# A fused attention and feed-forward kernel: layer 1's order on TensorE, and the start of the program, are rearranged

## The chip, the cores and the metric

The kernel runs on one core of a Trainium2 chip. The metric is device time in microseconds (us) of one execution, as the median of repeated runs. The core has TensorE (PE in the rows, its weight loads PEld), VectorE (DVE), ScalarE (ACT), GpSimd (POOL) and SyncE (SP), which here only issues transfers. Each engine works through its own instruction list in order; they meet at semaphores.

## The reference

Sixteen sequences of 512 tokens and 128 channels go through one attention block and one feed-forward block, each with its input added and normalised over the channels:

```python
normed = rms_norm(x, gamma)
q, k, v = normed @ w_q * 16**-0.5, *split(normed @ w_kv)     # 8 heads of 16
q, k = taylor(q), taylor(k)                                  # 1, x, x_i x_j / sqrt 2
out = (q @ (k^T v)) / max(q . sum(k), 1e-5)                  # linear attention
x = layernorm(x + out @ w_out)
h = silu(x @ w1^T * s1) * (x @ w2^T * s2)                    # 128 -> 512
h = gelu(h @ h1^T * hs1); h = gelu(h @ h2^T * hs2)           # 512 -> 512, twice
x = layernorm(x + h @ w3^T * s3)                             # 512 -> 128
```

All arrays are fp32. The weights w1, w2, h1, h2 and w3 are drawn from -1, 0 and 1 and multiplied by 8.

## The kernel before, in words

One sequence is one batch. The work of a batch is cut into four stages, and step t of the program does front of batch t, middle of t-1, ffn of t-2 and tail of t-3. Steps 0, 1 and 2 are written out, steps 3 to 14 run in a loop of two steps per pass, and 15 to 18 are written out again. Within a step the instructions of every engine stand in an order fixed by hand (`step` of each engine). The table RING names, in order, the uses of four PSUM banks by front and middle; FPS does the same for the four banks of ffn and tail. From these tables each wait is worked out: who writes a bank waits until its last content was read.

Front: x is scaled (`xn`), transposed (`xT`), multiplied by w_kv and w_q (`kv0` to `kv3`, `qT`); nine products with 0/1 matrices (`sq0` to `sq8`) form sums of q that ScalarE squares into `phiT`; `state` gathers k and v. Middle: the state of the batch before is transposed (`stateT`, `restT`), applied to phiT (`apply_main`, `apply_rest`, into `acc0`, `acc1`), divided (`normalise`, into `att`), projected (`out`), and x1 is transposed for the ffn (`x1T`). Ffn: layer 1 has a gate product a_m and a linear product b_m for each m of 0 to 3; ScalarE's `silu` reads a_m, VectorE's `gate_mult` multiplies it with b_m, `gate_hi` and `gate_lo` split the result in two parts. Layers 2 and 3 (`two0` to `three3`) end in `gelu` on ScalarE and `gelu_tile` on VectorE; layer 4 writes `y`, and ScalarE's `copy_y` takes it out for `transpose_y` of the next step. b1 and y use the same bank.

An operand that must be more exact than the fast fp32r format is split into a rounded part (`_hi`) and a rest (`_lo`). Activations always have both. For the ffn weights the kernel forms both, sums the absolute rests (`weights_lo_sum`), and TensorE reads the largest sum into a register (`value_load`) and branches: if there is no rest, the third product of each tile is left out. The profiled run goes that way. The three parts of the weights (w1, w2, w3; h1; h2) are loaded into tiles that the steps use later for other things, so their rests must be formed before step 1 goes on.

## Time and profile before

| | us |
|---|---|
| Median of 3 runs | 604.39 (604.31 to 605.26) |
| Profiled execution | 604.67 |
| its span, first to last instruction | 602.9 |
| TensorE, VectorE, ScalarE, GpSimd busy in the span | 559.8, 492.6, 464.5, 145.0 |
| TensorE's granted clock, mean | 0.984 |

The busy time of an engine is the time in which at least one of its instructions ran. Matmuls overlap, so the distance from one start to the next is what a matmul takes from TensorE, not the length in its row. "issue" is time in which an engine waited for nothing that the profile shows.

### The profile page before, as it was taken

To read this page: it belongs to the slowest core of one execution; us is meant where nothing else is said; L and a number is where in the kernel's file an instruction comes from. 1 tells how busy PE (TensorE), PEld (TensorE's weight loads), DVE (VectorE), ACT (ScalarE), POOL (GpSimd) and SP (SyncE) were. 2 spreads that over 40 slices of the span, in tenths; PEclk is the share of its full clock that TensorE was granted. 3 is DMA by queue.
4 is the path that set the end of the run, shared out by engine and by line. 5 is a ranking of instruction groups with operands and counts; after the bars stand their busy time and mean duration, and the time that the engine had idled before them with its cause. 6 is when DMAs were issued, how large, how long until landed. Compare 5 with 4: busy or idle time off the path is not lost.

```text
span 602.9 us, 11637 instructions
## 1 busy us (share of the span) xinstructions
PE 559.8 (93%) x3729; PEld 412.3 (68%) x3729; DVE 492.6 (82%) x1018; ACT 464.5 (77%) x953; POOL 145.0 (24%) x218
## 2 busy tenths in 40 slices
PE   3655999999999999999999999999999999999994
PEld 2334686867768686877868686776868687686772
DVE  5984886979799797979889797979979797987664
ACT  4565788796969788796978879796977969697773
POOL 5522112213212221312312231231132132110100
PEclk9986999999999999999999999999999999999998
DMA  8000000000000000000000000000000000000000
GB/s 277 1 20 3 1 17 3 18 18 18 20 0 17 17 17 17 17 17 17 0 17 17 17 17 17 17 17 0 17 17 17 17 17 17 1 1 18 6 14 35
DMA packets 7368, 12.36 MB, mean 21 GB/s; under 512 B 817, under 2 KB 1841, under 8 KB 7345
## 3 DMA queue, kind: packets, MB, share of 16 engines
q1 hardware_dynamic: 7056, 11.93, 5.8%
q8 instruction: 14, 0.23, 0.2%
q10 hardware_dynamic: 288, 0.13, 0.1%
q14 instruction: 10, 0.07, 0.0%
HBM read 7.86 MB, written 4.19 MB: 20 GB/s over the span
## 4 chain that ended last, share of the span: by engine, by line
PE 64%; ACT 15%; issue 12%; DVE 7%; DMA 1%; SPq 0%; DVEq 0%; POOLq 0%; POOL 0%; ACTq 0%
PE fps L416 20%; PE fps L417 19%; ACT phiT L630 5%; PE ring L395 5%; PE ring L387 5%; PE ring L319 4%; PE ring L342 3%; ACT hid_hi L673 3%; PE ring L403 2%; ACT fps L674 2%; PE ring L326 2%; ACT wide L679 2%; DMA h<-in_h 1%; PE fps L459 1%; ACT x1T_hi L639 1%
## 5 line engine op out<-in xcount | busy, mean ns | idle before, releaser
L416 PE MATMUL fps<-hid_hi,w_hi 128*128 128x512 f32 x576 | 226.8, 394 | 2.4 <-DVE hid_lo L897 1.8
L417 PE MATMUL fps<-hid_lo,w_hi 128*128 128x512 f32 x576 | 226.4, 393 | 0.0
L416 PEld LDWEIGHTS fps<-hid_hi,w_hi 128*128 128x128 f32 x576 | 108.2, 188 | 26.8 <-DVE hid_lo L897 4.1
L673 ACT ACTIVATE hid_hi<-fps,col 128x512 fp32r<-128x512 f32 x128 | 88.2, 689 | 46.3 <-PE fps L417 46.0
L417 PEld LDWEIGHTS fps<-hid_lo,w_hi 128*128 128x128 f32 x576 | 108.3, 188 | 22.4
L897 DVE TENSOR_TENSOR hid_lo<-fps,hid_hi 128x512 fp32r<-128x512 f32 x128 | 87.0, 689 | 24.2 <-ACT fps L674 22.0
L630 ACT ACTIVATE phiT<-ring 128x512 f32<-128x512 f32 x128 | 73.6, 595 | 28.2 <-PE ring L342 28.2
L674 ACT ACTIVATE fps<-fps,col 128x512 f32<-128x512 f32 x128 | 84.4, 660 | 0.0
L883 DVE SCALAR_TENSOR_TENSOR h<-fps,col,gate_zo 128x512 f32<-128x512 f32 x64 | 47.9, 749 | 42.8 <-ACT gate_zo L660 41.4
L259 DVE TENSOR_TENSOR phi_k<-phi_k 128x896 f32<-128x896 f32 x64 | 70.0, 1098 | 1.8 <-ACT v_one L602 1.3
L342 PE MATMUL ring<-qT,sel 128*128 128x512 f32 x128 | 55.3, 442 | 13.6 <-issue 9.0
L416 PE MATMUL fps<-x1T_hi,w_hi 128*128 128x512 f32 x128 | 56.3, 440 | 5.4 <-ACT wide L679 5.4
L1043 POOL TENSOR_TENSOR k_mid<-phi_k,v_one 128x256 f32<-128x256 f32 x32 | 21.4, 667 | 163.1 <-ACT v_one L602 133.2
L660 ACT ACTIVATE gate_zo<-fps,col 128x512 f32<-128x512 f32 x64 | 45.8, 715 | 15.7 <-PE fps L417 15.6
L889 DVE TENSOR_TENSOR hid_lo<-h,hid_hi 128x512 fp32r<-128x512 f32 x64 | 44.0, 687 | 9.2 <-ACT hid_hi L665 7.2
L417 PE MATMUL fps<-x1T_lo,w_hi 128*128 128x512 f32 x128 | 50.4, 394 | 0.0
L1024 POOL TENSOR_TENSOR rn<-ssc,const 128x4 f32<-128x4 f32 x16 | 16.6, 1039 | 129.9 <-DVE ssc L782 129.9
L653 ACT ACT_TABLE_LOAD x33 | 42.3, 1283 | 2.3 <-PEq L1129 1.7
L602 ACT ACTIVATE phi_k<-ring 128x128 f32<-128x128 f32 (+1 forms) x128 | 24.7, 256 | 24.6 <-PE ring L319 24.4
L416 PEld LDWEIGHTS fps<-x1T_hi,w_hi 128*128 128x128 f32 x128 | 24.0, 188 | 28.0 <-issue 12.6
L665 ACT ACTIVATE hid_hi<-h 128x512 fp32r<-128x512 f32 x64 | 42.3, 661 | 1.0 <-DVE h L883 0.9
L342 PEld LDWEIGHTS ring<-qT,sel 128*128 128x128 f32 x128 | 24.8, 198 | 23.9 <-issue 13.3
(107 smaller groups left out, 939.3 us busy)
## 6 DMA issues: line engine op xcount, KB each, us to landing
x_b<-in_x SPq DMA_DIRECT2D x16, 256.0 KB, 2.5
out<-gate_zo SPq DMA_DIRECT2D x16, 256.0 KB, 2.0
h<-in_h SPq DMA_DIRECT2D x1, 1024.0 KB, 8.1
gate_zo<-in_h SPq DMA_DIRECT2D x1, 1024.0 KB, 10.7
wide<-in_w SPq DMA_DIRECT2D x3, 256.0 KB, 3.9
sel_raw<-in_sel SPq DMA_DIRECT2D x1, 384.0 KB, 8.5
w_qkv_raw<-in_w_kv SPq DMA_DIRECT2D x1, 128.0 KB, 2.7
const<-in_consts ACTq DMA_DIRECT2D x1, 115.0 KB, 3.0
```

What stands on the lines that cost most here:

```text
L259: return eng.tensor_tensor(out, fixed, moved, ALU.mult)
L342: mm = nc.tensor.matmul(ring[:, bank, :], sel[:, (f % 4) * P:(f % 4 + 1) * P], qT[f // 4][:, :], start=True, stop=True)
L416: nc.tensor.matmul(fps[:, bank, :], w_hi[:, o:o + P], hi, start=start, stop=False)
L417: mm = nc.tensor.matmul(fps[:, bank, :], w_hi[:, o:o + P], lo, start=False, stop=stop and not with_lo)
L630: op = nc.scalar.activation(phiT[:, f, :], ring[:, bank, :], ACT.Square)
L653: nc.scalar.activation(table_use[:, :], source, function)
L660: nc.scalar.activation(gate[:, m % 2, :], fps[:, bank_of(FPS, f"a{m}"), :], ACT.Silu, scale=s1_c[:, m:m + 1]).then_inc(f_free[bank_of(FPS, ...
L673: nc.scalar.activation(hid[1 - layer][0][:, m, :], fps[:, bank, :], ACT.Gelu, scale=scale)
L674: nc.scalar.activation(fps[:, bank, :], fps[:, bank, :], ACT.Gelu, scale=scale)\
L883: nc.vector.scalar_tensor_tensor(out=h32[:, m, :], in0=fps[:, bank_of(FPS, b), :], scalar=s2_c[:, m:m + 1], in1=gate[:, m % 2, :], op0=ALU ...
L889: nc.vector.tensor_tensor(hid[0][1][:, m, :], h32[:, m, :], hid[0][0][:, m, :].bitcast(F32), ALU.subtract).then_inc(split_ready, 1)
L897: nc.vector.tensor_tensor(lo, fps[:, bank, :], hi.bitcast(F32), ALU.subtract)\
```

## The change

In the loop, TensorE does layer 1 as a0 b0 a1 b1, the three transposes, a2 b2 a3 b3, then `apply_main`, `apply_rest` and `transpose_y` in one piece, and then kv0 and kv1; before, the transposes and the two applies stood between the pairs of layer 1. ScalarE takes out the state and y of the step before first, then does silu 0, sq7, sq6, silu 1 and the copies of the transposed states; before, it copied sq6, sq7 and y ahead of silu 0, in that order. VectorE does phi_k 0 later.

In steps 0 to 2, no rests of weights are formed. The weights have a tile of their own (`w_raw`). ScalarE sums the lower 16 bits of each weight's pattern; TensorE adds these sums over the partitions with one small product, VectorE adds three numbers, and TensorE branches on the result. If it isn't zero, the products are done in full fp32 from `w_raw`. In step 0 ScalarE copies `sel`, and VectorE rounds no weights. `state`, `sq6` and `sq7` of batch 1 move behind the first half of layer 1 of step 2, and h1 is loaded behind `sel` and the second x.

```diff
@@ RING
-    ("stateT", MIDDLE, 0), ("restT", MIDDLE, 1), ("xT", FRONT, 2), ("kv0", FRONT, 3), ("acc0", MIDDLE, 0),
-    ("acc1", MIDDLE, 1), ("kv1", FRONT, 2), ("kv2", FRONT, 3), ("out", MIDDLE, 0), ("qT", FRONT, 1), ("kv3", FRONT, 2),
+    ("stateT", MIDDLE, 0), ("restT", MIDDLE, 1), ("xT", FRONT, 2), ("acc0", MIDDLE, 0), ("acc1", MIDDLE, 1),
+    ("kv0", FRONT, 3), ("kv1", FRONT, 2), ("kv2", FRONT, 3), ("out", MIDDLE, 0), ("qT", FRONT, 1), ("kv3", FRONT, 2),
@@ SyncE
             load_ffn_weights(0, (o1, w1t), (o2, w2t), (o3, w3t))
-            load_ffn_weights(1, (oh1, h1t))
             sp.dma_start(sel_raw[:, :], sel_d).then_inc(sel_loaded, 16)
             peeled(step, 0)
+            load_ffn_weights(1, (oh1, h1t))
             load_ffn_weights(2, (oh2, h2t))
@@ TensorE, product
-                mm = nc.tensor.matmul(fps[:, bank, :], w_hi[:, o:o + P], lo, start=False, stop=stop and not with_lo)
-                if with_lo:
-                    mm = nc.tensor.matmul(fps[:, bank, :], w_lo[:, o:o + P], hi, start=False, stop=stop)
-                return mm
+                if in_full:
+                    nc.tensor.matmul(fps[:, bank, :], w_raw[:, o:o + P], hi.bitcast(F32), start=start, stop=False)
+                    return nc.tensor.matmul(fps[:, bank, :], w_raw[:, o:o + P], lo.bitcast(F32), start=False, stop=stop)
...
@@ TensorE, step
+                    if is_step(t, 2):
+                        for part in range(3):
+                            pe.wait_ge(w_hi_ready[part], 1)
                     if ffn:
                         layer1(t, 0, in_full)
+                        layer1(t, 1, in_full)
+                    if is_step(t, 2):
+                        state(1)
+                        sums_of_q(1, 6)
+                        sums_of_q(1, 7)
                     if middle:
                         transpose_state(t)
-                    if ffn:
-                        layer1(t, 1, with_lo)
-                    if middle:
                         transpose_rest(t)
                     if front:
                         transpose_x(t)
                     if ffn:
                         layer1(t, 2, in_full)
+                        layer1(t, 3, in_full)
                     if middle:
                         apply_main(t)
-                    if ffn:
-                        layer1(t, 3, with_lo)
-                    if front:
-                        project_kv(t, 0)
-                    if middle:
                         apply_rest(t)
                     if tail:
                         transpose_y(t)
                     if front:
+                        project_kv(t, 0)
                         project_kv(t, 1)
@@ TensorE, the start
             pe.wait_ge(consts_loaded, 16)
-            pe.wait_ge(qkv_w_ready, 7)
...
                 apply_main(1)
+                apply_rest(1)
                 project_kv(1, 0)
-                apply_rest(1)
                 project_kv(1, 1)
+                pe.wait_ge(lo_sums_ready, 3)
+                nc.tensor.matmul(fps[0:1, 3, 0:3], half_c, lo_sums[:, :], start=True, stop=True)\
+                    .then_inc(lo_sums_added, 1)
...
-                pe.wait_ge(lo_max_ready, 1)
-                nc.tensor.transpose(fps[0:1, 3, 0:P], lo_max[:, :], ident).then_inc(lo_max_T, 1)
...
-                for f in (0, 1, 8, 2, 3):
-                    sums_of_q(1, f)
                 transpose_x1(1, 0)
-                sums_of_q(1, 4)
-                sums_of_q(1, 5)
-                state(1)
-                sums_of_q(1, 6)
-                sums_of_q(1, 7)
+                for f in (0, 1, 8, 2, 3, 4, 5):
+                    sums_of_q(1, f)
@@ ScalarE
+                low = w_raw[:, a:b].bitcast(mybir.dt.uint16).rearrange("p (n two) -> p n two", two=2)[:, :, 0]
+                nc.scalar.activation(unused[:, 0:b - a], low, ACT.Copy, accum_out=lo_sums[:, part:part + 1])\
+                    .then_inc(lo_sums_ready, 1)
...
             square(0, 0)
+            weights_low_bits(0)
...
             def step(t, par, front, middle, ffn, tail):
-                if ffn:
+                if is_step(t, 2):
                     silu(t, 0)
                 if middle:
-                    ring_copy(t, "stateT", w_main[:, :], ring[:, bank_of(RING, "stateT"), 0:2 * P], half_c)
+                    state_copy(t - 1)
+                if tail:
+                    copy_y(t - 1)
+                if ffn and not is_step(t, 2):
+                    silu(t, 0)
+                if middle:
+                    square_sums(t - 1, 7, 6)
                 if ffn:
                     silu(t, 1)
                 if middle:
+                    ring_copy(t, "stateT", w_main[:, :], ring[:, bank_of(RING, "stateT"), 0:2 * P], half_c)
                     ring_copy(t, "restT", w_rest[:, :], ring[:, bank_of(RING, "restT"), 0:2 * P])
                 if front:
                     x_hi(t)
                 if is_step(t, 0):
+                    act.wait_ge(sel_loaded, 16)
+                    nc.scalar.activation(sel[:, :], sel_raw[:, :], ACT.Copy).then_inc(sel_ready, 1)
+                if is_step(t, 1):
+                    weights_low_bits(2)
                     a, b = w_parts[0]
+                    nc.scalar.activation(w_hi[:, a:b], w_raw[:, a:b], ACT.Copy).then_inc(w_hi_ready[0], 1)
-                if is_step(t, 1):
-                    weights_lo_sum(0)
...
                 if is_step(t, 1):
-                    weights_lo_sum(1)
-                    weights_lo_sum(2)
+                    x1_hi(t)
...
+                if is_step(t, 0):
+                    weights_low_bits(1)
                 if middle:
                     load_table(ACT.Silu)
-                if front:
-                    ring_copy(t, "state", st[:, :, :].rearrange("p g f -> p (g f)"),
-                              ring[:, bank_of(RING, "state"), 0:2 * FEAT])
-                    square_sums(t, 6, 7)
-                if ffn:
-                    copy_y(t)
@@ VectorE, step
                     gate_mult(t, 1)
+                if front:
+                    x_lo(t)
+                if ffn:
                     gate_lo(t, 0)
-                if front:
-                    x_lo(t)
-                if ffn:
                     gate_mult(t, 2)
...
-                if front:
-                    phi_k_main(t, 0)
...
                     gelu_tile(t, 0, 0)
+                if front:
+                    phi_k_main(t, 0)
...
@@ VectorE, first_step
                 x_lo(0)
-                round_weights(dve, nc.vector, 1)
                 phi_k_main(0, 0)
-                dve.wait_ge(sel_loaded, 16)
-                nc.vector.tensor_copy(sel[:, :], sel_raw[:, :]).then_inc(sel_ready, 1)
                 q_lo(0)
@@ VectorE, second_step
-                split_weights(dve, nc.vector, 1)
+                round_weights(dve, nc.vector, 1)
+                x_lo(1)
                 round_weights(dve, nc.vector, 2)
-                split_weights(dve, nc.vector, 2)
-                x_lo(1)
+                normalise(1)
+                dve.wait_ge(lo_sums_added, 1)
+                nc.vector.tensor_reduce(lo_sum[:, :], fps[0:1, 3, 0:3], AX.X, ALU.add).then_inc(lo_sum_ready, 1)
                 phi_k_main(1, 0)
-                dve.wait_ge(w_lo_ready[0], 1)
-                normalise(1)
...
@@ GpSimd
             normed_x(0, 0)
-            split_weights(pool, nc.gpsimd, 0)
             peeled(step, 0)
```

## Rows read from the trace of the kernel before

**Rows 1.** The page: busy time, share of the span and instructions by engine.

```profile
PE 559.8 (93%) x3729; PEld 412.3 (68%) x3729; DVE 492.6 (82%) x1018; ACT 464.5 (77%) x953; POOL 145.0 (24%) x218
```

**Rows 2.** The waits: total us, times, longest.

```profile
PE fps L416 <- ACT wide L679: 5.4, 13, 0.4
```

**Rows 3.** Timeline, TensorE, one loop step: start us, length us, instruction, [idle before].

```profile
265.69 0.40 PE L416 MATMUL fps<-x1T_hi,w_hi 128*128 128x512 f32 x1
...
266.75 0.48 PE L416 MATMUL fps<-x1T_hi,w_hi 128*128 128x512 f32 x1
267.06 0.40 PE L417 MATMUL fps<-x1T_lo,w_hi 128*128 128x512 f32 x1
267.86 0.50 PE L416 MATMUL fps<-x1T_hi,w_hi 128*128 128x512 f32 x1 [0.41 <-ACT wide L679]
268.20 0.40 PE L417 MATMUL fps<-x1T_lo,w_hi 128*128 128x512 f32 x1
...
268.65 0.60 PE L311 MATMUL ring<-const,xn 128*128 128x128 f32 x4
...
272.54 0.39 PE L416 MATMUL fps<-x1T_hi,w_hi 128*128 128x512 f32 x1
...
300.28 0.40 PE L416 MATMUL fps<-x1T_hi,w_hi 128*128 128x512 f32 x1
```

**Rows 4.** Timeline, ScalarE, the same step.

```profile
266.16 1.07 ACT L630 ACTIVATE phiT<-ring 128x512 f32<-128x512 f32 x2
267.11 0.70 ACT L679 ACTIVATE wide<-fps,col 128x512 f32<-128x512 f32 x1
...
268.61 0.72 ACT L660 ACTIVATE gate_zo<-fps,col 128x512 f32<-128x512 f32 x1
```

**Rows 5.** Timeline, VectorE, the fill.

```profile
11.69 4.66 DVE L249 CAST w_hi<-h 128x512 fp32r<-128x512 f32 x4 [1.33 <-DMA h<-in_h]
...
18.69 0.68 DVE L800 TENSOR_TENSOR qT<-ring,qT 64x512 fp32r<-64x512 f32 x1
...
36.00 1.31 DVE L817 STREAM_TRANSPOSE wide<-ring 128x512 f32<-128x512 f32 x2
...
46.72 0.28 DVE L987 TENSOR_REDUCE lo_max<-fps 1x1 f32<-1x128 f32 x1
```

**Rows 6.** Timeline, TensorE, the fill.

```profile
24.04 3.81 PE L359 MATMUL ring<-phi_k,v_one 128*32 128x153 f32 x64
...
30.84 1.93 PE L387 MATMUL ring<-phiT,w_main 128*32 128x512 f32 x16
...
39.56 1.13 PE L403 MATMUL ring<-w_o,att 128*128 128x128 f32 x8 [2.44 <-issue]
...
42.18 0.41 PE L567 MATMUL fps<-const,lo_max 128*1 128x128 f32 x1
51.57 1.19 PE L342 MATMUL ring<-qT,sel 128*128 128x512 f32 x2 [8.97 <-issue]
...
55.90 2.29 PE L359 MATMUL ring<-phi_k,v_one 128*32 128x153 f32 x64
...
68.41 0.39 PE L416 MATMUL fps<-hid_hi,w_hi 128*128 128x512 f32 x1
```

**Rows 7.** Timeline, VectorE, the loop step of rows 3.

```profile
269.37 0.75 DVE L883 SCALAR_TENSOR_TENSOR h<-fps,col,gate_zo 128x512 f32<-128x512 f32 x1 [0.19 <-ACT gate_zo L660]
```

**Rows 8.** The DMA issue under way at 3.1 us: KB each, us to landing.

```profile
wide<-in_w SPq DMA_DIRECT2D x1, 256.0 KB, 4.9
```

**Rows 9.** Timeline, ScalarE, the fill.

```profile
9.04 0.60 ACT L608 ACTIVATE xnT_hi<-ring 128x512 fp32r<-128x512 f32 x1 [5.06 <-PE ring L311]
...
14.45 0.59 ACT L622 ACTIVATE qT<-ring 64x512 fp32r<-64x512 f32 x1 [0.71 <-PE ring L326]
...
31.24 1.48 ACT L648 ACTIVATE hid_lo<-w_lo 128x1536 fp32r<-128x1536 f32 x1
```

**Rows 10.** Stretch by engine: PE, PEld, DVE, ACT, POOL busy, PEclk, DMA, GB/s.

```profile
45.00:52.00 7.00, 0.43 (x1) 0.47 (x2) 5.04 (x10) 0.00 (x0) 1.68 (x3) 0.50 0.01 2
```

More of the change, by code:

```diff
@@ L187, in build @@
         qkv_w_ready = sem("qkv_w_ready")
-        w_hi_ready, w_lo_ready = ([sem(f"{n}{part}") for part in range(3)] for n in ("w_hi_ready", "w_lo_ready"))
-        lo_sums_ready, lo_max_ready, lo_max_T, lo_max1_ready = (
-            sem(n) for n in ("lo_sums_ready", "lo_max_ready", "lo_max_T", "lo_max1_ready"))
+        w_hi_ready = [sem(f"w_hi_ready{part}") for part in range(3)]
+        lo_sums_ready, lo_sums_added, lo_sum_ready = (sem(n) for n in ("lo_sums_ready", "lo_sums_added", "lo_sum_ready"))
         sq_ready, ss_ready, ssc_ready, rn_ready, xn_ready = (
@@ L316, in project_kv @@
                     pe.wait_ge(ring_free[bank_of(RING, "xT")], read(RING, t, "xT"))
+                    if is_step(t, 0):
+                        pe.wait_ge(qkv_w_ready, 7)
                 bank_wait(RING, ring_free, t, f"kv{j}")
@@ L412, in transpose_x1, with product, layer1 @@
                 mm.then_inc(f_full, 1)
-            def product(bank, o, hi, lo, start, stop, with_lo):
+            def product(bank, o, hi, lo, start, stop, in_full):
+                if in_full:
+                    nc.tensor.matmul(fps[:, bank, :], w_raw[:, o:o + P], hi.bitcast(F32), start=start, stop=False)
+                    return nc.tensor.matmul(fps[:, bank, :], w_raw[:, o:o + P], lo.bitcast(F32), start=False, stop=stop)
                 nc.tensor.matmul(fps[:, bank, :], w_hi[:, o:o + P], hi, start=start, stop=False)
-                mm = nc.tensor.matmul(fps[:, bank, :], w_hi[:, o:o + P], lo, start=False, stop=stop and not with_lo)
-                if with_lo:
-                    mm = nc.tensor.matmul(fps[:, bank, :], w_lo[:, o:o + P], hi, start=False, stop=stop)
-                return mm
-            def layer1(t, m, with_lo):
+                return nc.tensor.matmul(fps[:, bank, :], w_hi[:, o:o + P], lo, start=False, stop=stop)
+            def layer1(t, m, in_full):
                 for what, o in ((f"a{m}", o1), (f"b{m}", o2)):
@@ L427, in layer1, with hidden @@
                         pe.wait_ge(f_free[bank_of(FPS, "x1T")], read(FPS, t - 1, "x1T"))
-                    product(bank_of(FPS, what), o + m * P, x1T[0][:, :], x1T[1][:, :], True, True, with_lo)\
+                    product(bank_of(FPS, what), o + m * P, x1T[0][:, :], x1T[1][:, :], True, True, in_full)\
                         .then_inc(f_full, 1)
-            def hidden(t, what, o, wide, src, made_by, m, tiles, with_lo):
+            def hidden(t, what, o, wide, src, made_by, m, tiles, in_full):
                 for k in tiles:
@@ L440, in hidden, with layer2, layer3, layer4 @@
                     mm = product(bank_of(FPS, what), o + k * wide + m * P, hid[src][0][:, k, :],
-                                 hid[src][1][:, k, :], k == 0, k == KT - 1, with_lo)
+                                 hid[src][1][:, k, :], k == 0, k == KT - 1, in_full)
                     if k == KT - 1:
                         mm.then_inc(f_full, 1)
-            def layer2(t, m, tiles, with_lo):
-                hidden(t, f"two{m}", oh1, HID, 0, None, m, tiles, with_lo)
-            def layer3(t, m, tiles, with_lo):
-                hidden(t, f"three{m}", oh2, HID, 1, "two", m, tiles, with_lo)
-            def layer4(t, tiles, with_lo):
-                hidden(t, "y", o3, D, 0, "three", 0, tiles, with_lo)
+            def layer2(t, m, tiles, in_full):
+                hidden(t, f"two{m}", oh1, HID, 0, None, m, tiles, in_full)
+            def layer3(t, m, tiles, in_full):
+                hidden(t, f"three{m}", oh2, HID, 1, "two", m, tiles, in_full)
+            def layer4(t, tiles, in_full):
+                hidden(t, "y", o3, D, 0, "three", 0, tiles, in_full)
             def transpose_y(t):
@@ L532, in step @@
                     if ffn:
[L533 to L534 removed]
+                        layer3(t, 3, (2, 3), in_full)
+                        layer4(t, (0,), in_full)
                     if front:
@@ L704, in step @@
                     gate_hi(t, 2)
+                    gate_hi(t, 3)
                 if front:
                     copy_kv(t, 0)
-                if ffn:
-                    gate_hi(t, 3)
-                if front:
                     copy_kv(t, 1)
@@ L744, in step @@
                     square_sums(t, 3)
-                if middle:
+                if middle and not is_step(t, 1):
                     x1_hi(t)
@@ L908, in step @@
                 if ffn:
+                    gate_lo(t, 0)
                     gate_mult(t, 2)
```

91 lines of the change are left out of this document (37 added, 54 removed).

## The prediction

> **What bounds the kernel now.** I read the page first: TensorE is busy 93% of the span [rows 1], so the time is TensorE's work plus its gaps. The waits tell where the gaps of the loop are: one place has 13 of them, a layer 1 product held by ScalarE's copy of y [rows 2]. Then the timeline of one step. It runs from one a0 to the next, 265.69 to 300.28, 34.59 us [rows 3]. In it b1 starts 0.80 after the product before, where 0.23 is the pace, and the next takes 0.34: the wait costs 0.57 + 0.11 = 0.68. Elsewhere the step has no wait on TensorE. ScalarE is the one that is late: it does sq6 and sq7 at 266.16 and y at 267.11, for 0.70 [rows 4].
>
> The fill is another matter. TensorE waits for VectorE's q_lo, which stands behind the rounding of h1 (11.69, 4.66 long) and starts at 18.69 [rows 5]. Later TensorE stands idle for 8.97 before 51.57 [rows 6]: the lone maximum is ready at 46.72 + 0.28 = 47.00 [rows 5], and from there 4.57 pass in the register load and the branch. Layer 2 of the first ffn begins at 68.41 [rows 6].
>
> **The loop, step by step.** y moves ahead of sq6, sq7 and silu 0, behind the copy of the state, which keeps its place. So y takes the place of sq6, 266.16, and ends at 266.86. b1 comes directly behind a0, b0 and a1, six products of 0.23, and wants to start at 265.69 + 1.38 = 267.07. The margin is 0.2, and the 0.68 goes.
>
> What is late next is the chain silu 1, gate_mult 1, b3, for b3 writes the bank that gate_mult 1 reads. ScalarE's starts are 0.57 apart behind y and silu and 0.48 behind a square [rows 4]: silu 0 at 266.73, sq7 at 267.30, sq6 at 267.78, silu 1 at 268.25, where it was 268.61 [rows 4]. It still has both squares ahead of it, but the copy of the transposed state is behind it now. gate_mult 1 starts at 269.0, for 0.75 [rows 7], and frees b3 at 269.8. TensorE leaves b1 at 267.53, does three transposes of eight pieces in all (0.7 to 0.9, an estimate from 0.60 for the last four [rows 3]) and wants b3 six products later, at 269.7 to 269.9. So apply_main is no longer there as cover, and the slack is about nothing: wherever silu 1 comes later by x, TensorE waits x. The third transpose waits for the copy of sq7, to 267.9, which is also when TensorE gets there. I charge 0.05 for both, between 0 and 0.4 (the two squares' spread of starts). apply_main waits for the copies of the transposed states; they stand where they stood or earlier, within 0.6 behind silu 1, and layer 1 ends at 270.3.
>
> Changes of kind on TensorE: behind transposes an fp32r product takes 0.31 instead of 0.23 [rows 3]. Before there are four such returns (after the state's transpose, the other two, apply_main, transpose_y) and two entries into 32-column products; after, two returns and one entry. Three changes less at 0.08 to 0.11 (the restart above) give 0.24 to 0.33; I take 0.28. A step saves 0.68 + 0.28 - 0.05 = 0.91, with bounds 0.5 and 1.0. The 13 steps that show the wait save 11.8, between 6.5 and 13. Step 16 has no such wait; it gets the 0.28 and a normalise that no longer stands behind phi_k 0: 0.5, between 0.2 and 0.8.
>
> At no cost: x_lo, phi_k 0, gate_hi 3 and kv0 swap places within VectorE's, ScalarE's and TensorE's lists. phi_k 0 stands ahead of gelu_tile 1 but no longer ahead of normalise, so VectorE's list up to gelu_tile 1 is as long as before; were its cover gone, phi_k would cost its length, about 1.1 a step by my reading. ScalarE waits for TensorE in the middle of each step, so no lag adds up over steps. SyncE's x load waits for the same read of `out`, its store for the same out_ready.
>
> **The fill, step by step.** (a) x_hi 0 now stands behind the low-bit sum of w1, w2 and w3, and that waits for w3: issued at 3.08, 4.9 to landing [rows 8], so 7.98. The absolute sum of the same 1536 columns took 1.48 [rows 9]. Reading 16-bit halves 4 bytes apart isn't in the trace: between half and double of that, and I take 1.48, the nearest row. x_hi starts at 9.5 where it was 9.04 [rows 9], 0.4 later. q's copy follows 5.41 behind it [rows 9], at 14.9, and ends at 15.5. VectorE has no rounding and no copy of sel ahead of q_lo any more, so q_lo starts at 15.5 where it was 18.69: **3.2 earlier**. The copy of sel goes to ScalarE, where it waited for TensorE. sel is issued ahead of h1, so that 384 KB instead of 1408 KB follow w3; it has until about 11 to land. TensorE's removed wait at the very start (qkv_w_ready) is hidden, since x_hi is bound by w3. The rest follows q_lo: apply_main from 30.84 to 27.6 [rows 6]. The low-bit sum of h1 fills ScalarE's wait for state 0.
>
> (b) apply_rest comes directly behind apply_main: 27.6 + 1.85 + 1.93 = 31.4. VectorE's second transpose of normalise needs that; the pair starts as if at 30.75 instead of 36.00 [rows 5]. The rounding of h1 and h2 fits into VectorE's time before, and the copies of w1 to w3 into ScalarE's. project_out moves from 39.56 to 34.3: **5.25 earlier**. What GpSimd did for the rests leaves it idle; nobody waits.
>
> (c) Before, the maximum outlasts TensorE's work, whose last piece starts at 42.18 [rows 6]. Now the sum is ready before project_out, and TensorE comes to the branch at 42.2 - 5.25 = 36.9. The register load and the branch stay at 4.57: the first product comes at 41.5 where it was 51.57, **10.1 earlier**. Every instruction of TensorE is queued behind it; ScalarE and VectorE wait with it.
>
> The Trainium skill (Runtime: NRT & Kernel Launch, Instruction fetch mechanics) says that a taken branch to a target out of the prefetched pages has to fetch it before execution goes on. The trace has 4.57 there; by that rule none of it goes away, it only moves. Were it hidden, the sum would be 4.57 better.
>
> (d) Behind the branch there is more to fit: the transposes of x1 (0.6 to 0.8) stand ahead of the sums, x1_hi ahead of ScalarE's squares, and silu 0 behind a table load that ends at about 49.2. Laid out by the rows' lengths, a0 comes at 46.2, state 1 at 48.1, the third layer 1 product at 52.9 and layer 2 at 59.4, an estimate: 17.9 from the branch, where it was 68.41 - 51.57 = 16.84. So 1.05 is given back, and 9.05 stays.
>
> (e) TensorE's clock. The granted clock was 0.50, 1.2 of 2.4 GHz, after the sparse stretch before the branch [rows 10], and a state takes 3.81 or 2.29 by the level [rows 6]. State 1 comes 6.6 behind the restart instead of 4.3 [rows 6], but with a break before it; the applies of step 1 come 3.2 earlier. At the lower level state 1 costs 1.5 more, half of layer 1 up to 1.8, or the applies 3.7. I charge 1.0 of 0 to 4.
>
> The Trainium skill (TensorE: Matmul & The Clock Gate, What's actually happening) has the half clock as the default that activity releases, watched independently of the kernel's start. That speaks against counting on the full level in a fill with breaks; with the full level throughout, the fill would be worth 9.05.
>
> The fill is worth 8.05. Bounds: 3.6 (lower clock, 16-bit reads at double) and 10.1 (full clock, w3 and its sum in time, x_hi 1.0 earlier).
>
> **Sum.** 8.05 + 11.8 + 0.5 = 20.4. The profiled execution took 604.67, its span of 602.9 and 1.8 around it, 0.28 over the median: 604.67 - 20.4 = 584.3, and as a median 604.39 - 20.4 = **584.0 us**.
>
> **The rivals.**
>
> Cold fill: the applies of step 1, or what follows the branch, run at 1.2 GHz. For it: the level did fall [rows 10]. Against: the long breaks get shorter. 3 more than charged: 587.0. Chance 0.18.
>
> The tight chain takes back more: b3 is 0.45 late in each step (0.3 to 0.6), since its distance from a0 shrinks from 272.54 - 265.69 = 6.85 to 4.1 [rows 3]. 584.0 + 13 x 0.4 = 589.2. Against it: [rows 4, 7] put gate_mult 1's end where TensorE arrives. 0.12.
>
> Only the fill works, because b1 waits for ScalarE as before: 604.4 - 8.05 = 596.3. 0.04.
>
> Slower: if the gate chain needed the old 6.85 from a0, TensorE would wait 2.75 at b3: 13 x (2.75 - 0.96) = 23.3, less 8.55 of the fill and step 16: 619.1. It decides from 20.4 / 13 = 1.6 more than forecast per step. Nothing in [rows 4, 7] comes near. 0.03.
>
> The change doesn't see that the weights are exact, and each product runs in full fp32, far over 604. Weights of -8, 0 and 8 have no low bits set: 0.01.
>
> The forecast itself: 0.62, within 581 to 586.5. Range for 8 in 10: 579.5 to 589.5. Against 0.2%, about what this measurement can tell from no change: faster 0.95, same 0.01, slower 0.04.
>
> **What would show it.** No wait on y's copy in layer 1 and a step of 33.7. q_lo at 15.5, project_out at 34.3, the first product behind the branch at 41.5, layer 2 of step 2 at 59.4 to 61. A wait of over 0.3 at b3 or at the third transpose: the chain was tighter than read. ScalarE idle ahead of the copy of sel or of x_hi beyond 9.5: w3 or sel landed late, and (a) shrinks. Layer 1 of step 2 at half the pace: the clock.

## The result and the profile after

The changed kernel takes 583.74 us (median of 4 runs, 583.27 to 585.66) where the kernel before takes 604.83 (604.31 to 605.46) on the same chip: ratio 0.9661 [0.9648, 0.9673]. The forecast was 584.0. The profiled execution below took 585.66, the longest of the four, with a span of 583.9; step (e) of the section on the prediction says what is special about it. Line numbers shift: the products are L408 and L409 (L416 and L417 before), x1's transposes L400 (L411), project_out L392 (L403), gate_mult L878 (L883), y's copy L671 (L679), silu L652 (L660).

The page, busy line of the engines, and the group of the layer 1 products with the idle time before them (last column):

```profile
PE 554.3 (95%) x3730; PEld 414.3 (71%) x3730; DVE 479.5 (82%) x1008; ACT 465.2 (80%) x954; POOL 145.9 (25%) x215
...
L408 PE MATMUL fps<-x1T_hi,w_hi 128*128 128x512 f32 x128 | 53.7, 420 | 0.1
```

Against [rows 1], TensorE's busy time is 5.5 less and its share 2 points more. The number of products is the same but for one. Over the twelve loop steps that are compared below TensorE was busy for 410.49 of 415.47 us and is now busy for all of 404.59: the idle 4.98 is gone, and so are 5.90 of busy time, because after a wait or a change of kind the products start further apart, and there are fewer of both. The wait of [rows 2] is gone: layer 1 has 0.1 of idle time in all.

One step of the loop on TensorE, to be held against [rows 3]:

```profile
254.60 0.40 PE L408 MATMUL fps<-x1T_hi,w_hi 128*128 128x512 f32 x1
...
255.99 0.39 PE L408 MATMUL fps<-x1T_hi,w_hi 128*128 128x512 f32 x1
...
258.76 0.46 PE L408 MATMUL fps<-x1T_hi,w_hi 128*128 128x512 f32 x1
259.06 0.40 PE L409 MATMUL fps<-x1T_lo,w_hi 128*128 128x512 f32 x1
259.38 1.92 PE L376 MATMUL ring<-phiT,w_main 128*32 128x512 f32 x16
261.12 1.90 PE L384 MATMUL ring<-restq,w_rest 128*32 128x512 f32 x16
262.95 0.66 PE L448 MATMUL fps<-const,wide 128*128 128x128 f32 x4
```

b1 (255.99) starts 1.39 behind a0 (254.60), at the bare pace of six products of 0.23. b3 (258.76) is followed by its second product after 0.30 instead of 0.23: that 0.07 is all that the tight chain, which the prediction priced among its rivals, takes. From one transpose_y to the next it is 33.72 over twelve steps (94.33 to 498.92), before 34.62.

ScalarE and VectorE in the same step, against [rows 4] and [rows 7]:

```profile
255.07 0.68 ACT L671 ACTIVATE wide<-fps,col 128x512 f32<-128x512 f32 x1
...
256.21 1.09 ACT L617 ACTIVATE phiT<-ring 128x512 f32<-128x512 f32 x2
257.16 0.72 ACT L652 ACTIVATE gate_zo<-fps,col 128x512 f32<-128x512 f32 x1
```

```profile
257.91 0.75 DVE L878 SCALAR_TENSOR_TENSOR h<-fps,col,gate_zo 128x512 f32<-128x512 f32 x1 [0.80 <-ACT gate_zo L652]
```

y starts 0.47 behind a0 and ends 0.24 before b1 wants its bank. gate_mult 1 ends at 258.66 where b3 starts at 258.76.

The fill on ScalarE and VectorE, against [rows 9] and [rows 5]:

```profile
8.30 1.48 ACT L636 ACTIVATE hid_lo<-w_raw 128x1536 fp32r<-128x1536 uint16 x1 [4.15 <-DMA w_raw<-in_w]
...
9.79 0.58 ACT L595 ACTIVATE xnT_hi<-ring 128x512 fp32r<-128x512 f32 x1
```

```profile
15.80 0.68 DVE L795 TENSOR_TENSOR qT<-ring,qT 64x512 fp32r<-64x512 f32 x1 [1.89 <-ACT qT L609]
...
31.56 1.58 DVE L812 STREAM_TRANSPOSE wide<-ring 128x512 f32<-128x512 f32 x2 [1.97 <-PE ring L384]
...
35.21 0.11 DVE L971 TENSOR_REDUCE lo_sum<-fps 1x1 f32<-1x3 f32 x1
...
40.27 1.72 DVE L830 TENSOR_SCALAR x<-x1p,mv,rstd 128x128 f32<-128x128 f32 x4
```

The fill on TensorE, against [rows 6]:

```profile
27.02 3.36 PE L376 MATMUL ring<-phiT,w_main 128*32 128x512 f32 x16
30.08 2.28 PE L384 MATMUL ring<-restq,w_rest 128*32 128x512 f32 x16
...
35.39 1.13 PE L392 MATMUL ring<-w_o,att 128*128 128x128 f32 x8 [1.17 <-issue]
...
37.28 0.28 PE L308 MATMUL ring<-w_qkv_hi,xnT_lo 128*128 128x264 f32 x1
42.05 1.11 PE L400 MATMUL fps<-const,x 128*128 128x128 f32 x4 [4.49 <-DVE x L830]
...
47.34 0.63 PE L408 MATMUL fps<-x1T_hi,w_hi 128*128 128x512 f32 x1
...
50.88 2.44 PE L348 MATMUL ring<-phi_k,v_one 128*32 128x153 f32 x64
```

The number the branch needs is there at 35.32, before project_out. The first product behind the branch starts at 42.05, where it was 51.57. What released it is VectorE's `x`, which is x1, and not TensorE's own sequencer. Layer 2 of step 2 starts at 61.85, where it was 68.41.

The spans add up: 602.9 - 583.9 = 19.0 = 6.56 (start of layer 2) + 1.27 (from there to the first transpose_y, 33.75 before and 32.48 after) + 10.88 (twelve steps) + 0.3 (from the last transpose_y of these steps to the end).

### The profile page after: what moved, and what is told of

It reads as the page before. It is cut to its first block, busy times and chain, and to the rows that moved or that the text cites. A ratio compares the mean times of both kernels' runs of the same rounds, so it can differ in the third digit from the quotient of the medians.

```text
span 583.9 us, 11628 instructions
## 1 busy us (share of the span) xinstructions
PE 554.3 (95%) x3730; PEld 414.3 (71%) x3730; DVE 479.5 (82%) x1008; ACT 465.2 (80%) x954; POOL 145.9 (25%) x215
## 4 chain that ended last, share of the span: by engine, by line
PE 83%; issue 3%; DVE 2%; ACT 1%; POOL 0%; POOLq 0%; DVEq 0%
PE fps L408 25%; PE fps L409 25%; PE ring L348 5%; PE ring L331 5%; PE ring L376 5%; PE ring L384 4%; PE ring L308 4%; PE ring L392 2%; PE ring L315 2%; PE fps L448 1%; PE ring L298 1%; PE fps L400 1%; DVE h L878 1%; PE ring L334 1%; PE ring L366 1%
## 5 line engine op out<-in xcount | busy, mean ns | idle before, releaser
L408 PE MATMUL fps<-hid_hi,w_hi 128*128 128x512 f32 x576 | 226.6, 393 | 2.1 <-DVE hid_lo L892 1.4
L409 PE MATMUL fps<-hid_lo,w_hi 128*128 128x512 f32 x576 | 226.4, 393 | 0.0
L408 PEld LDWEIGHTS fps<-hid_hi,w_hi 128*128 128x128 f32 x576 | 108.2, 188 | 26.3 <-DVE hid_lo L892 3.7
L409 PEld LDWEIGHTS fps<-hid_lo,w_hi 128*128 128x128 f32 x576 | 108.3, 188 | 22.5
L892 DVE TENSOR_TENSOR hid_lo<-fps,hid_hi 128x512 fp32r<-128x512 f32 x128 | 88.2, 689 | 26.3 <-ACT fps L666 23.4
L878 DVE SCALAR_TENSOR_TENSOR h<-fps,col,gate_zo 128x512 f32<-128x512 f32 x64 | 47.9, 748 | 35.9 <-ACT gate_zo L652 32.5
L408 PE MATMUL fps<-x1T_hi,w_hi 128*128 128x512 f32 x128 | 53.7, 420 | 0.1
L409 PE MATMUL fps<-x1T_lo,w_hi 128*128 128x512 f32 x128 | 51.4, 401 | 0.0
L652 ACT ACTIVATE gate_zo<-fps,col 128x512 f32<-128x512 f32 x64 | 46.3, 723 | 0.1
L348 PE MATMUL ring<-phi_k,v_one 128*32 128x153 f32 x1024 | 37.0, 295 | 0.0
L348 PEld LDWEIGHTS ring<-phi_k,v_one 128*32 128x32 f32 x1024 | 31.5, 110 | 6.5 <-issue 5.7
```

The source lines that it names most:

```text
L348: mm = nc.tensor.matmul(ring[32 * hh:32 * hh + 32, bank, g * FEAT:(g + 1) * FEAT], v_one[:, j, 4 * g + hh, :], phi_k[:, j, 4 * g + hh, 0:F ...
L408: nc.tensor.matmul(fps[:, bank, :], w_hi[:, o:o + P], hi, start=start, stop=False)
L409: return nc.tensor.matmul(fps[:, bank, :], w_hi[:, o:o + P], lo, start=False, stop=stop)
L652: nc.scalar.activation(gate[:, m % 2, :], fps[:, bank_of(FPS, f"a{m}"), :], ACT.Silu, scale=s1_c[:, m:m + 1]).then_inc(f_free[bank_of(FPS, ...
L878: nc.vector.scalar_tensor_tensor(out=h32[:, m, :], in0=fps[:, bank_of(FPS, b), :], scalar=s2_c[:, m:m + 1], in1=gate[:, m % 2, :], op0=ALU ...
L892: nc.vector.tensor_tensor(lo, fps[:, bank, :], hi.bitcast(F32), ALU.subtract)\
```

## The experiments

The first separates the loop from the fill; the others take single steps of the prediction apart. Each ratio is against the kernel before, run beside that experiment (its medians lie between 604.60 and 605.27), so between experiments the ratios compare better than the times.

**The loop order alone.** The kernel before with the new order of the loop on all engines; the rests of the weights, the maximum, the branch and the order of the squares behind it as before, except that apply_rest stands ahead of kv0 in step 1 too. Its core, TensorE's part:

```diff
                     if ffn:
                         layer1(t, 0, with_lo)
+                        layer1(t, 1, with_lo)
                     if middle:
                         transpose_state(t)
-                    if ffn:
-                        layer1(t, 1, with_lo)
...
                         layer1(t, 2, with_lo)
-                    if middle:
-                        apply_main(t)
-                    if ffn:
                         layer1(t, 3, with_lo)
-                    if front:
-                        project_kv(t, 0)
                     if middle:
+                        apply_main(t)
                         apply_rest(t)
                     if tail:
                         transpose_y(t)
                     if front:
+                        project_kv(t, 0)
                         project_kv(t, 1)
```

> The kernel before with the new order of the loop alone (TensorE, ScalarE, VectorE), and the old start of the program, but for apply_rest that stands ahead of kv0 in step 1 too. By my account the step falls from 34.6 to 33.7 and the time to 604.4 - 11.8 - 0.5 = 592.1 (591 to 593). Rival: the two parts overlap, the old fill's idle time had hidden part of the loop's gain or the other way round; then this run and the fill's 8.05 don't add up to the changed kernel's time, and it comes out at under 590 or over 595.

Measured: 593.62 (592.39 to 594.07), ratio 0.9813 [0.9795, 0.983]; period 33.71, layer 2 of step 2 at 70.42. The period is as expected, the time is 1.5 above the expected 592.1 and outside its 591 to 593, but in neither of the rival's ranges. By the times the loop order is worth 11.2 here and the rest of the change 593.6 - 583.7 = 9.9. By the places in the span it divides otherwise: layer 2 starts 2.0 later than in the kernel before (70.42 against 68.41), and behind it 12.7 are gained, of the span's 10.7. The 2.0 has a cause in VectorE's list:

```profile
37.73 1.09 DVE L259 TENSOR_TENSOR phi_k<-phi_k 128x896 f32<-128x896 f32 x1 [3.45 <-ACT v_one L597]
```

kv0 now stands behind apply_rest, but in this step VectorE still does phi_k 0 ahead of normalise. It waits 3.45 for kv0's copies, where it waited 1.33 before (34.99), and normalise and project_out come later with it: project_out at 42.49 instead of 39.56. Two smaller things add to it: the fill began 0.64 later (x_hi 0 at 9.68 instead of 9.04), and apply_main took 3.28 instead of 1.93. The run on phi_k below shows the same trap in the loop. No run has the new fill with the old loop.

**The changed kernel again**, unchanged, in five runs.

> The changed kernel itself once more, as the measure for the runs beside it. My account (loop 11.8, fill 8.05, step 16 0.5) gives 604.4 - 20.4 = 584.0. A second profile of it also tells how much of the fill hangs on where TensorE's granted clock changes: the first had layer 2 of step 2 at 61.85, with half of layer 1 and most of apply_main at the lower level. If the clock explains the 1.5 us that the fill gave less than I said, a profile in which these run at the full level has it 1.5 to 3 us earlier; if not, it stays at 61.5 to 62.

Measured: 584.02 (581.8 to 585.67), ratio 0.9665 [0.9638, 0.9691]; span 581.1. The period is the same 33.72; its fill is not that of the first profile. TensorE, the same three places:

```profile
26.10 1.92 PE L376 MATMUL ring<-phiT,w_main 128*32 128x512 f32 x16
...
32.77 1.13 PE L392 MATMUL ring<-w_o,att 128*128 128x128 f32 x8 [1.17 <-issue]
...
39.44 1.12 PE L400 MATMUL fps<-const,x 128*128 128x128 f32 x4 [4.48 <-DVE x L830]
```

The first apply takes 1.92 instead of 3.36, because the granted clock differs. The windows of the first profile, then of this one (PE, PEld, DVE, ACT and POOL busy, then the granted clock):

```profile
27.00:31.00 4.00, 3.98 (x24) 1.40 (x28) 2.03 (x5) 3.79 (x4) 0.00 (x0) 0.57 0.01 2
...
44.00:48.00 4.00, 3.41 (x9) 2.20 (x8) 4.00 (x5) 3.96 (x8) 0.00 (x0) 0.50 0.00 0
```

```profile
27.00:31.00 4.00, 3.83 (x37) 1.65 (x29) 3.45 (x9) 3.52 (x8) 0.00 (x0) 1.00 0.02 6
...
44.00:48.00 4.00, 3.86 (x9) 2.81 (x9) 1.68 (x3) 3.97 (x8) 2.04 (x2) 0.50 0.00 0
```

From apply_main to project_out it is 8.37 in the first and 6.67 here: 1.70, with the same work between, so by the clock. kv0 starts 0.88 earlier here (10.26), since w3's low bits can be summed from 7.42 instead of 8.30. Behind the branch both run at 0.50.

**No branch.** TensorE goes straight into the loop of exact weights. The choice between the two loops is left out.

```diff
-            lo_bits = pe.value_load(lo_sum[:, :].bitcast(mybir.dt.int32))
-            with pe.If(lo_bits != 0):
-                second_step_sums()
-                steps_from_2(pe, steps_with(True))
-            with pe.Else():
-                second_step_sums()
-                steps_from_2(pe, steps_with(False))
+            second_step_sums()
+            steps_from_2(pe, steps_with(False))
```

> The changed kernel without the register load and the branch: TensorE always takes the short version (the choice is left out). By my step (c) the 4.57 us stand on the path, and the time is 584 - 4.6 = 579.2. Rival, from the first profile: TensorE's first product behind the branch, at 42.05, is released by x1, which is ready at 41.99, so x1's chain on VectorE has taken the branch's place, and leaving the branch out gives 0 to 0.3 us: 583.5.

Measured: 583.29 (582.77 to 583.85), ratio 0.9647 [0.9631, 0.9663]. Step (c) of the prediction, which put the time at 579.2, falls, and the rival holds. TensorE here:

```profile
33.23 1.13 PE L392 MATMUL ring<-w_o,att 128*128 128x128 f32 x8 [1.18 <-issue]
...
39.99 1.09 PE L400 MATMUL fps<-const,x 128*128 128x128 f32 x4 [4.58 <-DVE x L825]
```

From project_out to x1's transposes it is 6.76 without a branch and 6.66 with it. The branch costs nothing in the changed kernel that can be told from the spread of its runs (584.02 beside it, with overlapping intervals).

**Squares ahead of x1.** If x1 is what the first product waits for, something else can go first, and shows when the branch is done.

```diff
             def second_step_sums():
+                sums_of_q(1, 0)
+                sums_of_q(1, 1)
                 transpose_x1(1, 0)
-                for f in (0, 1, 8, 2, 3, 4, 5):
+                for f in (8, 2, 3, 4, 5):
```

(In ScalarE's step 1 the rounding of x1 moves behind the squares of these two sums.)

> The changed kernel with sq0 and sq1 of batch 1 ahead of x1's transposes behind the branch (ScalarE's copies in the same order). These two need only q_lo, ready at 40.3, so the first product behind the branch shows when the branch itself lets TensorE go. If the branch takes 4.57 from the end of kv3 (37.56), it is 42.1, as now, and the branch and x1's chain end together; if it is much shorter once its condition is long ready, 40.3. The time moves by less than 1 us either way: ScalarE's squares start 0.5 to 1 earlier, x1 0.9 later.

Measured: 582.92 (581.62 to 583.3), ratio 0.9634 [0.9618, 0.9651]. Its interval and that of the changed kernel overlap. TensorE, and the piece of VectorE that released it:

```profile
36.18 0.28 PE L308 MATMUL ring<-w_qkv_hi,xnT_lo 128*128 128x264 f32 x1
38.46 0.73 PE L331 MATMUL ring<-qT,sel 128*128 128x512 f32 x2 [2.00 <-DVE qT L797]
40.94 0.66 PE L400 MATMUL fps<-const,x 128*128 128x128 f32 x4 [1.75 <-DVE x L832]
```

```profile
34.10 0.11 DVE L973 TENSOR_REDUCE lo_sum<-fps 1x1 f32<-1x3 f32 x1
...
37.72 0.68 DVE L797 TENSOR_TENSOR qT<-ring,qT 64x512 fp32r<-64x512 f32 x1
```

Even here TensorE is released by VectorE (q's low half, done at 38.40) and not by the branch. So register load and branch were over by 38.46: at most 2.0 behind the end of the last product before them (36.46), and at most 4.25 behind the moment the sum was ready (34.21). How long they take when TensorE has nothing else to do, two runs that keep the old way to the branch show beside the 4.57 of the kernel before. With the loop order alone the maximum is ready at 50.14 and the first product starts at 54.23, 4.09 behind it; in the run below that moves only y's copy in the kernel before it is 47.51 and 51.61, 4.10. So 4.57 is no constant. Counted from the number, 4.1 fit under the 4.25; counted from the last product (36.46 + 4.1 = 40.56) they don't. The delay therefore doesn't start only when TensorE's queued products are done. Whether it runs beside them or is shorter here, the runs don't separate.

**The low-bit sums later.** Part 0's sum goes from the front of x_hi 0 to the end of step 0, part 1's into step 1.

```diff
                 if is_step(t, 1):
+                    weights_low_bits(1)
                     weights_low_bits(2)
...
                 if is_step(t, 0):
-                    weights_low_bits(1)
+                    weights_low_bits(0)
...
-            weights_low_bits(0)
```

> The changed kernel with the low-bit sum of w1, w2, w3 moved from the very start to the end of step 0, and that of h1 into step 1. My step (a) says that x_hi 0 is held by w3's landing and this sum: it would start at 8.65 (behind the transposes) instead of 9.79, q_lo at 14.7 instead of 15.8, and all of the fill comes 1.1 us earlier, 1.5 with the state copy that no longer waits for a long sum: 582.5. Rival: the three sums now end too late in step 1 and hold kv0's copy and the branch: no gain or slower, 583.7 to 585.

Measured: 583.44 (582.38 to 584.66), ratio 0.9655 [0.9638, 0.9673]. x_hi starts at 8.70 and TensorE's sums of q at 15.47 (16.54 in the first profile of the changed kernel, 15.62 in the second), project_out at 33.19. What this order gains up front is mostly gone by project_out, and the time can't be told from that of the changed kernel.

**ScalarE's old order in the changed loop.** State, sq6, sq7, y, silu 0, silu 1.

```diff
                 if middle:
                     state_copy(t - 1)
+                if middle:
+                    square_sums(t - 1, 6, 7)
                 if tail:
                     copy_y(t - 1)
                 if ffn and not is_step(t, 2):
                     silu(t, 0)
-                if middle:
-                    square_sums(t - 1, 7, 6)
```

> The changed kernel with ScalarE's old order at the start of a step: state, sq6, sq7, y, silu 0. TensorE keeps its new order. By my account y then ends 1.0 us later (two copies of 0.48), b1 wants to start 1.38 behind a0 and waits about 0.8, plus 0.11 for the restart: the step goes back to 34.6 and the time to 584 + 13 x 0.9 = 595.7. Rival: the gate chain behind it is what sets the step, and costs more than b1's wait (silu 1 and gate_mult 1 late as well): over 598. Second rival: the wait is taken up again by slack before b3: 588 to 592.

Measured: 593.15 (591.59 to 595.25), ratio 0.9808 [0.9777, 0.9839]; period 34.47. The forecast was 595.7 with a step of 34.6, so the direction and the cause hold and the size is a little less; neither rival's range holds. The waits have the old row again:

```profile
PE fps L408 <- ACT wide L671: 8.2, 13, 0.7
```

13 waits of 0.63 and the 0.11 of the restart make 0.74, the 0.75 by which the period grew. With layer 1's pairs together, the new order of ScalarE's list, in which y comes ahead of the squares, is worth 0.75 of the loop's 0.90.

**Only ScalarE's order, in the kernel before.** y ahead of sq6 and sq7, everything else as before the change.

> The kernel before with nothing changed but y's copy ahead of sq6 and sq7. b1 no longer waits (0.68 a step), but silu 0 and gate_mult 0 stay where they were, and b2, which comes 0.68 earlier, needs gate_mult 0's end at 269.18 against 268.87: it gets 0.3 to 0.4 back as a wait. 604.6 - 13 x 0.35 = 600. If the whole 0.68 stays: 595.8. If y's place were of no account: 604.6.

Measured: 602.62 (602.25 to 603.32), ratio 0.9969 [0.9957, 0.9982]; period 34.42, 0.20 less. The expectation was 600, with 0.35 a step. The wait on y is off the list and has come back as two smaller ones. TensorE behind the third transpose:

```profile
267.34 0.60 PE L311 MATMUL ring<-const,xn 128*128 128x128 f32 x4
267.80 0.50 PE L416 MATMUL fps<-x1T_hi,w_hi 128*128 128x512 f32 x1
268.14 0.40 PE L417 MATMUL fps<-x1T_lo,w_hi 128*128 128x512 f32 x1
268.58 0.50 PE L416 MATMUL fps<-x1T_hi,w_hi 128*128 128x512 f32 x1
```

a2 comes 0.46 behind the transpose where [rows 3] have 0.36 (268.65 to 269.01), its products are 0.34 apart instead of 0.31, b2 comes 0.44 behind and not 0.23, and its products are again 0.34 apart, not 0.23: 0.45 of the 0.68 are back. In this order silu 0 still stands behind y and both squares. a2 takes the bank that silu 0 has read (to 267.75), b2 the bank that gate_mult 0 has read (to 268.53). Neither half of the change does it alone: y's place alone gives 0.20 a step, the rest of the loop's change without ScalarE's new order (the run before this one) 34.62 - 34.47 = 0.15, both 0.90.

**apply_main as cover.** In the changed kernel, a3 and b3 stand between apply_main and apply_rest, as before the change.

```diff
                     if ffn:
                         layer1(t, 2, in_full)
-                        layer1(t, 3, in_full)
                     if middle:
                         apply_main(t)
+                    if ffn:
+                        layer1(t, 3, in_full)
+                    if middle:
                         apply_rest(t)
```

> The changed kernel with layer 1's last pair (a3, b3) between apply_main and apply_rest, as it stood before. It prices the changes of kind: one entry (0.09), one return (0.11), and the 0.11 by which apply_rest followed apply_main faster in the first profile (1.74 instead of 1.85), less 0.07 of b3's wait: 0.24 a step in 15 steps, 583.8 + 3.6 = 587.4. If b3's chain in its tight place costs more than I saw, splitting gives it cover, and the time rises less or falls: 583 to 585.

Measured: 590.83 (589.17 to 593.99), ratio 0.9789 [0.9761, 0.9818], where 587.4 was expected; period 34.20, so the split costs 0.48 a step, twice the expected 0.24. TensorE and ScalarE:

```profile
256.93 0.39 PE L409 MATMUL fps<-x1T_lo,w_hi 128*128 128x512 f32 x1
257.44 1.92 PE L376 MATMUL ring<-phiT,w_main 128*32 128x512 f32 x16
259.29 0.50 PE L408 MATMUL fps<-x1T_hi,w_hi 128*128 128x512 f32 x1
259.63 0.40 PE L409 MATMUL fps<-x1T_lo,w_hi 128*128 128x512 f32 x1
```

```profile
256.96 0.43 ACT L591 ACTIVATE w_rest<-ring 128x256 f32<-128x256 f32 x1
```

b2's last product to apply_main is 0.51 where entering apply_main takes 0.32 in the changed kernel (259.06 to 259.38): 0.18 of waiting for w_rest, which ends at 257.39. The other 0.3 is changing kind: the two applies joined are 1.74 apart (259.38 to 261.12) and part with 1.85 (257.44 to 259.29), the product behind takes 0.34 instead of 0.23, and apply_rest is entered anew (0.32 instead of 0.23).

**phi_k back ahead of normalise.** One line of VectorE's list in the changed loop.

```diff
                     gate_lo(t, 3)
+                if front:
+                    phi_k_main(t, 0)
                 if middle:
                     normalise(t)
...
                     gelu_tile(t, 0, 0)
-                if front:
-                    phi_k_main(t, 0)
```

> The changed kernel, but in the loop VectorE does phi_k 0 of the next batch ahead of normalise, as before the change; it still stands ahead of the first gelu tile. The prediction's view: the list up to the gelu tile is as long either way, so the period stays at 33.72 within 0.05 and the time at 584 (within 1.5). Rival: normalise comes about 1.1 later in each step and with it att, project_out and x1, which layer 1 of the next step waits for; then TensorE waits where out or x1T stands, up to 1.1 a step, and the time is 590 to 598.

Measured: 596.3 (596.04 to 598.1), ratio 0.9862 [0.9846, 0.9877]: about 12 slower than the changed kernel (0.0197 to 0.0201 by the ratios); the mean period over twelve steps is 34.71, 1.0 more. The prediction's view falls. The time is the rival's, but by another chain. VectorE, then the waits of TensorE:

```profile
267.21 1.09 DVE L247 TENSOR_TENSOR phi_k<-phi_k 128x896 f32<-128x896 f32 x1 [0.98 <-ACT v_one L589]
...
277.34 0.69 DVE L892 TENSOR_TENSOR hid_lo<-fps,hid_hi 128x512 fp32r<-128x512 f32 x1
```

```profile
PE fps L408 <- DVE hid_lo L892: 9.8, 16, 0.9
```

VectorE waits 0.98 for the copies of kv0. TensorE makes kv0 and kv1 only behind transpose_y now, so phi_k has its input that much later, and everything behind phi_k in the list is late by it. att is late too, but project_out is not held up (6.66 behind transpose_y, 6.63 in the changed kernel). The first to wait is layer 3, for the third low half of the gelu. In the changed kernel that half is done at 274.30 and used at 274.76, so it has 0.46 to spare. Here it is done 1.14 later, counted from transpose_y, and the product that reads it starts 0.94 behind the one before it instead of 0.23 (277.14 to 278.08); with the 0.11 of the restart that is 0.82 of the 1.0. Where the rest is lost wasn't followed.

**Two edits joined:** the low-bit sums later and the squares ahead of x1.

> The changed kernel with two edits joined: the low-bit sums of part 0 and 1 one place later on ScalarE, and the sums of q of batch 1 for features 0 and 1 ahead of x1's transposes behind the branch. Alone they took 583.44 and 582.92 beside 584.02 for the changed kernel. If both gains are real they add up: 582.3. Rival: both are within the spread that the granted clock of the fill gives the changed kernel (581.8 to 585.7), and the joined kernel's interval takes in the ratio 0.9665 of the changed kernel: 583 to 584. Place to look: kv0 at 10.1 and sq0 at 15.5, the first product behind the branch at 37.5 to 38.5, and the start of layer 2 of step 2 (59.16 and 58.19 alone).

Measured: 581.09 (580.8 to 581.57), ratio 0.96 [0.9587, 0.9613]: faster than the changed kernel, whose ratios were 0.9661 and 0.9665, and by more than the two edits gave alone (0.0065 against 0.0010 and 0.0031, all from 0.9665). TensorE's sums of q begin at 15.43, project_out at 33.38, the first product behind the branch at 37.50, and layer 2 of step 2 at 57.16 (59.08 and 61.85 in the changed kernel). In its profile the first half of layer 1 runs almost all at the full clock:

```profile
44.00:48.00 4.00, 4.00 (x61) 3.28 (x64) 2.44 (x5) 3.65 (x7) 1.58 (x2) 0.93 0.00 0
```

From a0 to the state behind b1 it takes 2.06 (44.30 to 46.36), against 3.53 (44.73 to 48.26) in the second profile of the changed kernel: 1.47 of the 1.92 by which its layer 2 starts earlier. But the edits aren't shown to be what brought that clock. The same window in the run with a3 and b3 between the applies, whose order up to this place is that of the changed kernel, and in the run with the squares ahead of x1:

```profile
44.00:48.00 4.00, 3.40 (x38) 2.53 (x41) 2.42 (x4) 3.97 (x7) 1.39 (x2) 0.91 0.00 0
```

```profile
44.00:48.00 4.00, 3.80 (x10) 2.82 (x9) 2.80 (x5) 3.97 (x8) 1.01 (x2) 0.50 0.00 0
```

The first has nothing to do for 4.47 ahead of x1's transposes and still goes from a0 to the state in 1.93; the low-bit run does it in 1.92. The second has its two sums of q in that stretch and takes 3.55. So the joined kernel is faster, in five runs that lie within 0.8 of each other, but one profile doesn't show why it beats the sum of its parts.

## Why the prediction was right, and where not

**The loop** was forecast at 0.91 a step and is 0.90. Of its three terms, the wait (0.68) went whole, and b3's wait is 0.07 where 0.05 was charged. That leaves 0.90 - 0.68 + 0.07 = 0.29 for the three changes of kind less, taken at 0.28; the split found 0.3 for putting an entry and a return back and parting the applies. The margin at b1 was 0.24, with 0.2 forecast. With steps 2 and 16 the loop is 10.88 + 1.27 + 0.30 = 12.45, against 12.3.

**"At no cost"** was right in its result, but its reason for phi_k 0 was wrong. I wrote that VectorE's list up to gelu_tile 1 is as long as before, and priced a lost cover at phi_k's length. I counted lengths and not inputs: kv0 and kv1 now come later, and phi_k in its old place costs 1.0 a step, more than the whole gain of the loop. Its move was a condition of that gain, not a bystander.

**(a)** x_hi was forecast at 9.5 and started at 9.79 and 8.90 in the two profiles; the spread is w3's arrival. The 16-bit sum took 1.48, the value taken from the 32-bit row. q_lo came at 15.80 against 15.5.

**(b)** project_out was forecast at 34.3. It came at 32.77 with the full clock and at 35.39 with the lower one under the applies. The term is right, and part of the clock charge belonged here.

**(c)** is the step that failed, though its number came out within 0.6 in the first profile: "The register load and the branch stay at 4.57: the first product comes at 41.5". It came at 42.05 and 39.44 in the two profiles, and without any branch it comes as far behind project_out (6.76, against 6.66 and 6.67). The number was ready at 35.32, and the 4.1 to 4.57 seen with TensorE idle would end before 40. What holds the product is the chain from att over project_out, x1 and its statistics, q's low halves, which VectorE does in between, and x1's scaling: 6.66 from project_out to the transposes. That the branch seemed to end at the same time (4.57 behind kv3's end at 37.56 would be 42.13) is a coincidence. I had the chain in hand and never laid it beside the branch. The Trainium skill (Runtime: NRT & Kernel Launch, Instruction fetch mechanics) says that a taken branch to a target out of the prefetched pages has to fetch it first; the prediction read this as a cost that only moves. No run here shows the fetch itself; the runs show that, with the number ready early, it needn't be on the path.

**(d) and (e)** From the first product behind the branch to layer 2 it is 19.80 and 19.64, where 17.9 and a clock charge of up to 1.8 were forecast. The run with the low-bit sums later has the same order behind the branch and its first half of layer 1 at the full clock: it takes 17.76 (40.43 to 58.19). So the layout of (d) was right within 0.2. From a0 to the state behind b1 the two profiles of the changed kernel take 3.54 and 3.53 and that run 1.92, so the lower clock costs 1.6 there. (e) was too small: 1.0 for all places, where 1.6 came in layer 1 in both profiles and 1.7 under the applies in one of them. One reading in (e) also doesn't hold as it stands: it took the 3.81 of state 0 in [rows 6] for the price of the lower level, but the granted clock of that stretch is given as 1.00 (24 to 28 us). The same 64 products have the slower pace there all the same.

The fill gave 6.56 and 9.33 in the two profiles; by the medians it is 21.1 - 12.45 = 8.6, with 8.05 forecast. w3's arrival and the clock spread it by 2.8, so the closeness of the sum is partly luck.

**The rivals.** The cold fill (587.0) is half there in the first profile, which ran 585.66. The tight chain, priced at 0.45 a step, took 0.07. The other three have nothing in any trace of the changed kernel.

## What to carry over

Where an edit moves work on one engine, look up for each instruction behind it not only how long the list is but when its inputs are made now: an innocent swap of one line (phi_k) decided about 12 us. Before pricing a branch or another fixed delay on the path, write down the second chain that ends at the same instruction; if the two are within a microsecond, removing either one is worth nothing. And two lists that feed each other (TensorE's order, ScalarE's order) may have to be changed together: here 0.20 and 0.15 a step apart, 0.90 joined.

## What the hardware showed unexpectedly

From the moment the number was ready to the first product behind the branch TensorE stood idle for 4.57 in the kernel before, and for 4.09 and 4.10 in two runs that keep the old way to the branch. When the number is ready while TensorE still has products to do, the branch is over at most 2.0 behind the last of them.

TensorE's granted clock fell to 0.50 (1.2 GHz) during the idle 4.5 ahead of x1's transposes in both profiles of the changed kernel, and it was at 0.57 under the applies (27 to 31 us) in one of these two profiles of the same program, where the other had 1.00. That alone spreads the fill by 1.7. How early it is back at 1.00 differs between runs with the same work there: half of layer 1 takes 3.5 in the changed kernel's two profiles and 1.93 in a run whose order up to that place is the same. Two sums of q in the idle stretch went with the full clock in one run (0.93) and with 0.50 in another. What decides it stays open.

The granted clock of a profile doesn't tell the pace everywhere. In the first 20 us it is given as 1.00 in the changed kernel's first profile while products of 512 columns start 0.42 to 0.43 apart (13.66, 14.08, 14.51), as they do behind the branch at 0.50, and not 0.23 as in the loop. In such a stretch the distance of the starts is the better witness.

Summing 16-bit halves that lie 4 bytes apart takes ScalarE as long as 32-bit words: 1.48 for 1536 columns. VectorE's scaling of x1 took 1.72 in the changed kernel's fill, where GpSimd works beside it, and 1.11 in the fill before; the cause wasn't tried apart.
